# Slot numbers ahead of the norm's sum, and twelve of sixteen scatters a turn sooner, in the gated memory of a vision tower

## What is computed

```python
def step(carry, inp):
    M, n, m = carry
    qt, kt, vt, li, lf, op = inp
    m_next = jnp.maximum(lf + m, li)
    i_s = jnp.exp(li - m_next)
    f_s = jnp.exp(lf + m - m_next)
    M = f_s[:, :, None] * M + i_s[:, :, None] * (vt[:, :, None] * kt[:, None, :])
    n = f_s * n + i_s * kt
    h_raw = jnp.einsum('bij,bj->bi', M, qt)
    denom = jnp.maximum(jnp.abs(jnp.einsum('bi,bi->b', n, qt))[:, None], 1e-06)
    h = jax.nn.sigmoid(op) * (h_raw / denom)
    return ((M, n, m_next), h)
...
idx = jnp.argmax(probs, axis=-1)
one_hot = jax.nn.one_hot(idx, E, dtype=jnp.float32)
pos = (jnp.cumsum(one_hot, axis=0) * one_hot).sum(-1).astype(jnp.int32) - 1
...
buf = jnp.zeros((E, C, D), dtype=h.dtype).at[idx, pos_safe].set(x, mode='drop')
```

## Time and profile before

| | |
|---|---|
| median of 3 runs | 3205.5 us (3203.17 to 3209.28) |
| profiled execution: its own time | 3203.23 us |
| its span, first to last instruction | 3201.0 us |
| granted TensorE clock, mean over the span | 0.962 of full speed |
| busy in the span | PE 87%, DVE 76%, ACT 68%, POOL 60% |
| one steady turn of the stage, 1004.0 to 1034.6: busy | PE 28.22, DVE 25.93, ACT 24.91, POOL 23.87 us; clock 1.00 |
| the stage's end, 1460 to 1545: busy | PE 29.78, DVE 19.89, ACT 9.85, POOL 65.06 us |

### The profile page before, as it was taken

The page is one execution under the profiler, slowest core; times in us unless marked ns, Lnnn a source line. Parts: engine busy times, 40 slices in busy tenths (PEclk is TensorE's granted clock), DMA queues, the critical chain, the costliest instruction groups (busy, mean ns, idle before and its releaser), DMA issues. The chain is left out here.

```text
span 3201.0 us, 68718 instructions
## 1 busy us (share of the span) xinstructions
PE 2796.7 (87%) x25818; PEld 1558.3 (49%) x25818; DVE 2419.8 (76%) x3224; ACT 2174.9 (68%) x3138; POOL 1914.1 (60%) x1191
## 2 busy tenths in 40 slices
PE   7999999969999999995499958799989898989897
PEld 5666666635555555553244413344444444444444
DVE  6888888858888888884387638787878787878783
ACT  6777777758888878872144437676777777777672
POOL 8888888811677777777200066666666665656531
PEclk9999999989999999996799959999999999999999
DMA  1111111111221222211444421112212121212111
GB/s 48 42 42 39 41 41 42 40 59 36 62 72 55 73 56 56 62 42 51 141 151 152 140 57 36 37 46 54 58 47 62 44 62 49 56 49 56 47 36 51
DMA packets 208269, 191.21 MB, mean 60 GB/s; under 512 B 76381, under 2 KB 163398, under 8 KB 207562
## 3 DMA queue, kind: packets, MB, share of 16 engines
q1 hardware_dynamic: 173850, 142.95, 15.4%
q0 software_dynamic: 25600, 26.01, 3.6%
q10 hardware_dynamic: 8496, 17.87, 1.5%
HBM read 99.08 MB, written 87.65 MB: 58 GB/s over the span
## 5 line engine op out<-in xcount | busy, mean ns | idle before, releaser
L2418 POOL DMA_INDIRECT E_row<-yb,P_gi x400 | 401.1, 1003 | 395.5 <-POOLq L93 302.0
L2425 POOL TENSOR_TENSOR E_w<-E_w,E_rs 128x1024 f32<-128x1024 f32 x200 | 393.8, 1969 | 406.4 <-DVE E_rs L2333 406.4
L689 POOL DMA_INDIRECT xb<-B_yt,P_gi x400 | 469.3, 1173 | 115.4 <-issue 113.8
L204 POOL TENSOR_TENSOR A_kmask<-A_ksb,A_pack_a 128x3584 f32<-128x3584 f32 x56 | 356.3, 6363 | 115.2 <-ACT A_ksb L374 115.2
L2218 ACT ACTIVATE E_w<-E_w 128x1024 f32<-128x1024 f32 x200 | 211.8, 1059 | 252.8 <-DVE E_w L2326 252.0
L2330 DVE TENSOR_REDUCE E_sm<-E_w 128x16 f32<-128x1024 f32 x200 | 243.9, 1220 | 138.7 <-ACT E_w L2218 136.9
L2318 DVE TENSOR_REDUCE E_mx<-E_lg 128x16 f32<-128x1024 f32 x200 | 237.6, 1188 | 63.0 <-PE E_lg L1983 62.9
L474 DVE COPY A_vbd<-A_v 128x512 f32<-128x512 f32 x336 | 215.6, 684 | 74.1 <-PE A_v L324 74.1
L2326 DVE TENSOR_TENSOR E_w<-E_lg,E_mx 128x1024 f32<-128x1024 f32 x200 | 244.1, 1220 | 4.6
L2014 PEld LDWEIGHTS E_wt<-S_pack_f,E_w 128*128 128x128 f32 (+1 forms) x1600 | 174.7, 141 | 139.5 <-issue 105.2
L1983 PE MATMUL E_lg<-S_wxs,E_yo 64*128 64x512 f32 x800 | 229.2, 649 | 9.7 <-DVE E_w L2326 9.6
(11 more groups left out here) (321 smaller groups left out, 6830.9 us busy)
## 6 DMA issues: line engine op xcount, KB each, us to landing
R_xs<-xb SPq DMA_DIRECT2D x57, 256.0 KB, 2.7
yb<-R_ys SPq DMA_DIRECT2D x57, 256.0 KB, 2.0
B_x<-h SPq DMA_DIRECT2D x25, 512.0 KB, 4.3
h<-B_hh SPq DMA_DIRECT2D x25, 512.0 KB, 3.2
A_xg<-in_xw SPq DMA_DIRECT2D x56, 224.0 KB, 2.5
h<-A_res ACTq DMA_DIRECT2D x56, 224.0 KB, 2.6
E_hx<-h SPq DMA_DIRECT2D x48, 256.0 KB, 2.9
out<-E_ob SPq DMA_DIRECT2D x96, 128.0 KB
```

Source lines behind the costliest of these rows:

```text
L204: nc.gpsimd.tensor_tensor(kmask[i % 2][:], bc(ksb[i % 2][:].unsqueeze(2), [128, J, H, Q]), bc(head_of_row[:].unsqueeze(1).unsqueeze(3), [1 ...
L689: pool.indirect_dma_start(out=xb, out_offset=bass.IndirectOffsetOnAxis(ap=routed.gi[0:k, c, b:b + 1], axis=0), in_=yt[c % LT][0:k, D * row ...
L2418: pool.indirect_dma_start(out=row[b % LR][:, k, i], out_offset=None, in_=yb, in_offset=bass.IndirectOffsetOnAxis(ap=idx[:, c, 2 * n + i:2 ...
L2425: TT(w3, w3, bc(rs[g % 3][:].unsqueeze(2), [128, 2 * SH, G]), ALU.mult).then_inc(w_done, 1)
```

## The change

Two places, in two engines' loops of the same stage. On GpSimd the scatters in front of age become images 12 to 15 of chunk t - 5 (four instead of five), and those behind mems become images 0 to 11 of chunk t - 4 (twelve instead of eleven): these twelve go one turn sooner, in the very turn in which VectorE computes their gi. On VectorE the steps `slots` and `numbers`, which write gi, move ahead of `norm_sum`.

```diff
                 for t in range(CHUNKS + 5):
                     at(weigh_keys, t - 1)
-                    at(scatter, t - 5, range(0, 5))
+                    at(scatter, t - 5, range(12, B))
                     at(age_memory, t - 2)
                     at(scale_memory, t - 1)
-                    at(scatter, t - 5, range(5, B))
+                    at(scatter, t - 4, range(0, 12))
...
                     at(own, t - 4)
+                    at(slots, t - 4)
+                    at(numbers, t - 4)
                     at(norm_sum, t - 1)
-                    at(slots, t - 4)
                     at(gate_out, t - 1)
-                    at(numbers, t - 4)
                     at(norm_weight, t - 1)
```

## The result

The change takes 3257.64 us (median of 4 runs, 3254.77 to 3259.78); the kernel before took 3207.39 beside it (4 runs, 3203.17 to 3215.81). The ratio is 1.0157, 95% interval 1.0144 to 1.0171: 50 us slower. The forecast was 3248.5 with a range of 3216 to 3270. The profiled execution has a span of 3252.4 us (before 3201.0), at a mean granted clock of 0.952 (before 0.962).

The account below looks back on a forecast made before the run. VectorE, nearly gapless in a ring with TensorE, was taken to bound the gated-memory stage; GpSimd had 2.0 us slack a turn. +53.8 - 10.8 = +43.0 on 3203.2 gives 3246.2, plus 2.3: 3248.5 us, range 3216 to 3270.

Parts of the forecast that it names:

- step (3), the ring: Gated-memory stage: twelve scatters waiting for this turn's gi close a ring through both engines; turn 33.13, not 30.57: +53.8 us.
- the milder rival: Scatter 2 slips in ahead of nq and kx beats cm; turn 31.86 us, +16 in all, 3222; chance 0.20.
- (1): VectorE from own to nq: slot and the cast wait for their predecessors, +0.22 us a turn, at most +0.26.
- (2): GpSimd's memory scaling: one scatter fewer in front of age, worth nothing as long as age waits for hh.
- TensorE's transposition: TensorE's transposition of the memory also waits for mems; costed at nothing, as VectorE has 9.9 us of its own work.
- (4): Stage's end: 64 scatters instead of 75 after the last scaling, -14.1, against the gi wait and new holds: -10.8 us.
- Not held: Scatters run freely beside VectorE's two-operand SBUF instructions, so twelve fit before kx: -6.8 us, 3199; chance 0.10.
- Harder: hh also catches a scatter behind kx, age 1.2 later, turn 34.3 us: +68 in all, 3273; chance 0.13.
- the granted clock: TensorE's granted clock might drop in the longer turns and make the size wrong; nothing was added for it.

Follow-up runs that it names:

- filled: The change plus two 512-column matmuls, never read, in TensorE's wait for yy each turn: 3257.21 us, ratio 1.0157 to the kernel before.
- the filled VectorE half: The kernel before with slot and gi moved ahead of nx, GpSimd as before, plus two unread 512-column matmuls in TensorE's wait for yy: 3218.36 us, ratio 1.0034.
- the memset: The kernel before with a small VectorE memset of a tile nothing reads, ahead of nx: 3222.80 us, ratio 1.0050.
- VectorE's half alone: The kernel before with only slot and gi moved ahead of nx, GpSimd's scatters as before: 3245.67 us, ratio 1.0130.

## Why the prediction was right, and where its sizes were off

Its step (3), the ring, is what happened. In us from the end of one gi cast, as forecast, with the clock filled (gi cast's end at 1012.37) and in the change (1008.17):

| | forecast | filled | change |
|---|---|---|---|
| cm starts | 18.57 | 18.65 | 20.30 |
| kx starts | 19.6 | 19.54 | 19.54 |
| kx ends | 23.16 | 23.11 | 21.92 |
| normed (po) starts | 23.02 | 23.26 | 24.28 |
| age starts | 29.06 | 29.18 | 28.89 |
| mems ends | 31.53 | 31.41 | 31.13 |
| next gi cast ends | 33.13 | 33.35 | 33.40 |

With the clock up, the forecast holds line by line. Its one wrong step there that costs time is that nth slips in behind age: nth is caught by mems too (1.26 us instead of 0.42), and ex begins only behind it, 0.22 later in all.

In most turns of the change the order of kx and cm is the other way round, as in the milder rival, but for another reason: the slow denominator brings arg 1.7 us later (5.04 against 3.35 of wait), cm comes at 20.30, and kx, which hangs on GpSimd's chain alone, is first. The turn is no shorter for it, for GpSimd's chain from the first scatter to mems has no gap: kx, no longer held, ends 1.2 earlier, but the scatter behind it is held by cm (2.83 us), and age comes at 28.89. The 1.7 us of TensorE lie beside this chain. They do so only up to a point. In five turns the denominator is on the lower level for its whole length (3.75 us), arg waits 6.0 to 6.4 us, and age again has about 0.5 us idle ahead of it; TensorE's chain is the longer one there, and from gi to gi it takes 33.6 to 34.0 us. One of them:

```profile
882.23 3.75 PE L711 MATMUL B_PD<-B_nq,B_pack_b 128*128 128x512 f32 x4 [2.67 <-DVE B_yy L1213]
```

```profile
901.63 1.04 POOL L682 TENSOR_TENSOR B_mem<-B_mem,B_g 128x512 f32<-128x512 f32 x1 [0.53 <-issue]
```

That is why the clock costs 28 us or more without the ring and some 5 with it.

**By the steps.** (1) VectorE's order was put at 0.22 us, at most 0.26, and is 0.35 at full clock (30.92 against 30.57): from own to nq the filled VectorE half takes 4.22 us where 4.09 was forecast, 0.09 of it because nx starts 0.17 behind the cast's start instead of 0.08. The larger miss is that the step took the turn to grow only by VectorE's own work: alone, the order lengthens TensorE's wait ahead of the denominator, and the clock falls behind it. Beside the ring hardly any of that is on the path. (2) One scatter fewer ahead of age "worth nothing as long as age waits for hh": the condition fell, as step (3) says itself; age now follows the scatters directly. (3) 21 turns were put at +2.56 each, 53.8; they took 63.4, 3.0 each. Of the 0.46 more, 0.22 is nth, and some 0.2 goes with the clock (33.65 against 33.43 in the mean of twenty turns). The parts don't add up exactly: the first of the 21 turns has 34.5, and the kernel before itself lost some 3 us in two turns in which its clock fell. TensorE's transposition, at nothing, holds: the filled change has it waiting 2.1 us at most for mems and keeps the turn. (4) The end was put at −10.8: it is −11.4, and −1.6 between the last kx and mems.

**The rivals.** *Not held* falls: the second scatter takes 1.99 us beside nq and the fourth 1.85 beside ls. Here the inference in the Trainium skill (SBUF — State Buffer, "Who interferes with whom"), that a tensor_tensor leaves GpSimd's descriptor writing alone, does not carry over to these scatters; nq is a tensor_tensor with both operands in SBUF, and it holds the scatter. Whether the scatter is held in writing its descriptors or in reading its row numbers from gi, no run here separates. *Milder*: its order came, its price did not. *Harder*: in the filled turn hh does catch a scatter (2.02 us), but in place of the one that normed was forecast to catch, and age is on time. What the prediction named as what could spoil the size, the granted clock, did drop, and cost little only because the ring was longer in most turns. The forecast had not weighed the one against the other; that part of its near hit is luck.

## What to carry to other kernels

Work that an in-order engine does for the next stage may be pulled one turn forward only as far as its inputs are already done when its place comes: twelve pulled forward with a wait on this turn's numbers, and VectorE's new order for them, cost 50 us, seven pulled forward behind four of the older chunk, whose inputs were long done, gained 9. Two costs that lie beside each other show only the larger one: take each out alone, here by filling TensorE's wait, before one of them is named as the cause. And where an engine waits in every turn of a tight loop, look at what its clock does behind that wait, even if the edit adds only a fraction of a microsecond to it.

## What the runs showed of the hardware

The clock's fall is not the same in every turn with the same wait. From 850 to 1400 the kernel before has TensorE waiting 2.38 to 2.54 us ahead of the denominator, and the denominator was slow in 2 of 18 turns (3.4 us instead of 1.96); with the memset (waits of 2.60) in 4 of 17; in VectorE's half alone (2.73 to 3.08) in 11 of 17; in the change (2.67 to 3.62) ScalarE waited for a slow denominator in 14 of 17. So the same wait, 2.73 us in VectorE's half, was followed by either level. In all of them TensorE was at full clock in the last 2 us ahead of the wait. With two matmuls inside the wait (0.4 to 1.4 us left of it in the filled runs) every denominator took 1.95 or 1.96 us.

The first scatter behind the wait on gi starts 0.80 us after the cast's end (1042.37 against 1041.57), where age stood 0.14 behind hh; nx holds that scatter longer than that, so it is free here.

A copy of 8 columns (B_tot, 0.15 us) stands 2.27 us behind kx: an instruction that is held pays for the one that it meets, however small it is itself.
